# Attention tables of both heads of a block built in its first half, and one of two value copies moved to VectorE

## What is computed

```python
q, k, v = cproj(Wq), cproj(Wk), cproj(Wv)        # complex, 16 heads of 64
qr, kr = q * phase, k * phase                    # rotation by cos and sin tables of the head
E = exp(clip(-mu * |t_i - t_j|, -30, 0))         # decay table of the head
s = Re(qr . conj(kr));  qn = |q|^2;  kn = |k|^2
V = sigma_sq / (2 mu) * (1 - E*E) + eta_sq + gamma_sq
maha = max(qn + E*E*kn - 2*E*s, 0) / V
logits = coef * log1p(maha / nu) - 32 * log(V)   # causal
out = softmax(logits) @ v;  x = x + [Re out, Im out] @ Wo
```

## Time and profile before

| | us |
|---|---|
| median of 3 runs (lowest, highest) | 1714.13 (1711.09, 1719.28) |
| the profiled execution | 1711.93 |
| its span, first to last instruction | 1710.1 |
| busy in the span: PE, DVE, ACT, POOL | 1650.9, 1488.8, 1457.8, 974.7 |
| even halves of the 8 blocks, together | 644.49 |
| odd halves, together | 576.27 |

### The profile page before, as it was taken

The page is one execution under the profiler, slowest core; times in us unless marked ns, Lnnn a source line. Parts: engine busy times, 40 slices in busy tenths (PEclk is TensorE's granted clock), DMA queues, the critical chain, the costliest instruction groups (busy, mean ns, idle before and its releaser), DMA issues. The chain is left out here.

```text
span 1710.1 us, 30987 instructions
## 1 busy us (share of the span) xinstructions
PE 1650.9 (97%) x9690; PEld 1334.7 (78%) x9690; DVE 1488.8 (87%) x3380; ACT 1457.8 (85%) x2924; POOL 974.7 (57%) x826
## 2 busy tenths in 40 slices
PE   5999988999999999999999999999999999999998
PEld 4787866877887888788788778878887887777876
DVE  6878887899899989988998998899899989977675
ACT  6677678999999999999999999999998998766765
POOL 3554556565556556655665566556565655345565
PEclk9999999999999999999999999999999999999999
DMA  6000032232222323232322223232222222100000
GB/s 175 1 1 1 1 102 66 67 80 62 75 60 78 78 59 81 57 87 50 87 66 65 72 72 75 51 87 62 75 66 72 66 63 60 25 1 13 13 8 18
DMA packets 49475, 98.21 MB, mean 57 GB/s; under 512 B 8096, under 2 KB 25760, under 8 KB 49312
## 3 DMA queue, kind: packets, MB, share of 16 engines
q1 hardware_dynamic: 49312, 96.23, 22.0%
HBM read 17.95 MB, written 5.24 MB: 14 GB/s over the span
## 5 line engine op out<-in xcount | busy, mean ns | idle before, releaser
L1482 POOL TENSOR_TENSOR early<-early 128x1024 f32<-128x1024 f32 x127 | 303.4, 2389 | 483.3 <-PE pS L1162 258.2
L654 POOL TENSOR_TENSOR hid_lo_d<-hid_d,hid_hi_d 128x512 fp32r<-128x512 f32 x176 | 231.4, 1315 | 218.7 <-ACT hid_hi_d L559 212.1
L1373 ACT ACTIVATE early<-early,qnorm 128x128 f32<-128x128 f32 (+3 forms) x512 | 246.5, 553 | 71.8 <-DVE early L1564 70.6
L1162 PE MATMUL pS<-early 128*128 128x128 f32 (+3 forms) x1024 | 297.6, 433 | 0.3 <-PEq L105 0.3
L1356 ACT ACTIVATE early<-early,nmax 128x128 f32<-128x128 f32 (+3 forms) x512 | 281.2, 560 | 13.4 <-DVE nmax L1551 12.5
L1560 DVE SCALAR_TENSOR_TENSOR pS<-pS,ek 128x1280 f32<-128x1280 f32 x128 | 191.0, 1492 | 60.7 <-PE pS L1162 59.8
L1162 PEld LDWEIGHTS pS<-early 128*128 128x128 f32 x1024 | 164.7, 191 | 96.0 <-issue 61.4
L1491 POOL TENSOR_TENSOR ek<-early 128x128 f32<-128x128 f32 (+3 forms) x256 | 216.3, 878 | 3.8 <-ACT early L1364 2.9
L1491 POOL TENSOR_TENSOR ek<-decay,early 128x128 f32<-128x128 f32 (+3 forms) x256 | 215.5, 876 | 2.4 <-DVE pS L1560 2.4
L1177 PEld LDWEIGHTS pV<-ones,early 128*128 128x128 f32 x1016 | 134.2, 193 | 60.8 <-issue 60.8
L1207 PE MATMUL pS<-ident,early 128*128 128x128 f32 x1280 | 169.0, 275 | 12.4 <-DVE early L1564 8.3
(11 more groups left out here) (395 smaller groups left out, 3953.3 us busy)
## 6 DMA issues: line engine op xcount, KB each, us to landing
early<-early SPq DMA_DIRECT2D x256, 256.0 KB, 3.6
early<-trig_d SPq DMA_DIRECT2D x64, 64.0 KB, 2.0
trig_d<-early SPq DMA_DIRECT2D x3, 1024.0 KB, 6.9
early<-in_w SPq DMA_DIRECT2D x3, 704.0 KB, 8.8
x_sb<-in_x SPq DMA_DIRECT2D x4, 512.0 KB, 8.4
early<-in_wqk SPq DMA_DIRECT2D x16, 128.0 KB, 3.5
cos<-trig_d SPq DMA_DIRECT2D x32, 64.0 KB, 2.2
sin<-trig_d SPq DMA_DIRECT2D x32, 64.0 KB, 2.0
```

Of the source, the lines that this page charges most:

```text
L654: g.tensor_tensor(hid_lo[:, par], hid[:, par], hid_hi[:, par].bitcast(F32), ALU.subtract).then_inc(lo_done, 1)
L1162: last = pe.matmul(s.pS[:, span(I)], rot[:, I * P:(I + 1) * P], rot[:, N:N + (I + 1) * P], start=True, stop=True)
L1373: last = a.activation(u[:, span(I)], u[:, span(I)], ACT.Relu, bias=qnorm[:, r % 2, I:I + 1])
L1482: g.tensor_tensor(rot[:], by_cos[:], crossed[:], ALU.add).then_inc(S["rot_done"], 1)
```

## The change

Two things change.

First, both heads that come next (the odd one of this block and the even one of the next block) are built in the even half. Each part has now a pair of places, one for each of the two. The decay argument of an even head gets a buffer of its own (`far_even`), because the table `decay[0]` is still in use, and is spread by four DMAs in place of three at r = 8; `lam` of the even heads has two buffers. The parameters are read where they lie, so the copy of them (L1509) is gone. The high part of the weights is cast on VectorE, no longer on ScalarE.

Second, `values_out` on ScalarE copies only the even head's values. The odd head's are copied by VectorE in `values_odd`, at the end of its step, after a wait for ScalarE's copy (`val_done`). TensorE's norms, which write the same banks, wait for both.

```diff
-        FRONT, EXP, EXPAND, LN, MASK = 1, 2, 3, 4, 6
+        FRONT, EXP, HALF, LOW, SQUARE, LN, MASK = (1, 2), (2, 3), (3, 6), (4, 7), (3, 5), (4, 6), (6, 7)
+        WEIGHTS, TRIG, EXPAND = (1, 5), (1, 9), (3, 8)
         def building(part, i, r):
-            if r % B != part:
-                return None
...
+            for off in (1, 2):
+                if r == part[off - 1] and i * 2 + off < H:
+                    return i * 2 + off
+            return None
+            def expand(h):
+                par = h % 2
                 wait(sp, S["decay_done"], h + 1)
+                wait(sp, S["t_done"], 2 * (h - 1) * B)
+                for I in range(TILES - par):
+                    sp.dma_start(decay[par][:, span(I)], far(h)[:, near(I)]).then_inc(expanded[par], 16)
...
                 if live(i, r - 2) and parity(r - 2) == 0:
                     wait(pe, S["val_done"], values_made(i, r - 2))
+                    wait(pe, S["val_odd_done"], values_made(i, r - 2))
...
             def build(part, h):
                 if part == EXP:
-                    a.wait_ge(S["w_in"], h * 16 + 16)
-                    wait(a, S["qk_done"], (h - 1) * B)
-                    a.activation(wqk[par][0][:], wqk_raw[:], ACT.Copy).then_inc(S["w_hi"], 1)
                     a.wait_ge(S["arg_done"], h + 1)
+                    a.activation(far(h), far(h), ACT.Exp).then_inc(S["decay_done"], 1)
...
             def values_out(i, r):
                 a.wait_ge(S["v_done"], values_made(i, r))
-                for h, val in enumerate((val_even[r % B % 3], val_odd[r % B])):
-                    last = a.activation(val[:].rearrange("p (j d) -> p j d", j=TILES),
-                                        s.pV[:].rearrange("p (j h d) -> p h j d", j=TILES, h=2)[:, h], ACT.Copy)
-                last.then_inc(S["val_done"], 1)
+                a.activation(val_even[r % B % 3][:].rearrange("p (j d) -> p j d", j=TILES),
+                             s.pV[:].rearrange("p (j h d) -> p h j d", j=TILES, h=2)[:, 0],
+                             ACT.Copy).then_inc(S["val_done"], 1)
...
+            def build_half(h):
+                v.wait_ge(S["w_in"], h * 16 + 16)
+                wait(v, S["qk_done"], (h - 1) * B)
+                v.tensor_copy(wqk[h % 2][0][:], wqk_raw[:]).then_inc(S["w_hi"], 1)
...
+            def values_odd(i, r):
+                v.wait_ge(S["val_done"], values_made(i, r))
+                wait(v, S["av_done"], i * 16 + r - 7)
+                v.tensor_copy(val_odd[r % B][:].rearrange("p (j d) -> p j d", j=TILES),
+                              s.pV[:].rearrange("p (j h d) -> p h j d", j=TILES, h=2)[:, 1]).then_inc(S["val_odd_done"], 1)
...
+                if live(i, r) and parity(r) == 0:
+                    values_odd(i, r)
```

More of the change, by code:

```diff
@@ L1069, in attention_phase, with lam, far, hp @@
         near = lambda I: slice((TILES - 1 - I) * P, N)
+        def lam(h):
+            return lam1[:] if h % 2 else lam_even[h // 2 % 2]
+        def far(h):
+            return decay[h % 2][:, span(TILES - 1)] if h % 2 or h == 0 else s.far_even
+        def hp(h, k):
+            return s.params[:, h, k:k + 1]
         HALVES = ((slice(0, N), ORDER[:2]), (slice(N, SW), ORDER[2:]))
@@ L1129, in load @@
                     sp.dma_start(sin[par][rows, :], s.trig_d[table, h]).then_inc(trig_in[par], 16)
-            def expand(i, off):
-                h, par = i * 2 + off, off % 2
+            def expand(h):
+                par = h % 2
                 wait(sp, S["decay_done"], h + 1)
-                far = decay[par][:, span(TILES - 1)]
-                for I in range(TILES - 1):
-                    sp.dma_start(decay[par][:, span(I)], far[:, near(I)]).then_inc(S["expanded"], 16)
+                apart(sp, S["sp_passed"])
+                wait(sp, S["t_done"], 2 * (h - 1) * B)
+                for I in range(TILES - par):
+                    sp.dma_start(decay[par][:, span(I)], far(h)[:, near(I)]).then_inc(expanded[par], 16)
             def a_step(i, r):
@@ L1330, in _, with build @@
         def _(a):
-            def build(part, i, off):
-                h, par = i * 2 + off, off % 2
+            def build(part, h):
                 if part == EXP:
-                    a.wait_ge(S["w_in"], h * 16 + 16)
-                    wait(a, S["qk_done"], (h - 1) * B)
-                    a.activation(wqk[par][0][:], wqk_raw[:], ACT.Copy).then_inc(S["w_hi"], 1)
                     a.wait_ge(S["arg_done"], h + 1)
-                    far = decay[par][:, span(TILES - 1)]
-                    a.activation(far, far, ACT.Exp).then_inc(S["decay_done"], 1)
+                    a.activation(far(h), far(h), ACT.Exp).then_inc(S["decay_done"], 1)
                 elif part == LN:
@@ L1343, in build @@
                         a.wait_ge(S["decay_done"], 1)
-                        a.activation(decay2[:], decay[0][:, span(TILES - 1)], ACT.Square).then_inc(S["decay2_done"], 1)
+                        a.activation(decay2[:], far(0), ACT.Square).then_inc(S["decay2_done"], 1)
                     a.wait_ge(S["decay2_done"], h + 1)
-                    wait(a, S["zred_done"], 2 * (h - 1) * B)
-                    a.activation(lam[par][:], decay2[:], ACT.Ln, bias=hp[par][:, A_PLUS_B:A_PLUS_B + 1],
-                                 scale=hp[par][:, NEG_A:NEG_A + 1]).then_inc(S["lnv_done"], 1)
+                    wait(a, S["zred_done"], 2 * (h - (1 if h % 2 else 3)) * B)
+                    a.activation(lam(h), decay2[:], ACT.Ln, bias=hp(h, A_PLUS_B), scale=hp(h, NEG_A)).then_inc(S["lnv_done"], 1)
             def soften(i, r):
@@ L1441, in a_step @@
                 if i == 0 and r == -1:
-                    build(LN, 0, 0)
+                    build(LN, 0)
                 if i == 0 and r == 0:
@@ L1456, in a_step @@
                     if building(part, i, r):
-                        build(part, i, building(part, i, r))
+                        build(part, building(part, i, r))
                 if live(i, r + 2):
@@ L1486, in spread @@
                 wait(g, S["decay_done"], i * 2 + r // B + 1)
-                wait(g, S["expanded"], 48 * (i * 2 + r // B))
+                wait(g, expanded[par], 48 * (i + r // 16 + 1) if par else 64 * (i + r // 16))
                 wait(g, S["norm_done"], n + 1)
@@ L1505, in _ @@
         def _(v):
[L1506 to L1512, removed]
@@ L1544, in peaks @@
-                v.wait_ge(S["lam_done"], i * 2 + r // B + 1)
+                n, h = i * 16 + r, i * 2 + r // B
+                v.wait_ge(S["lam_done"], h + 1)
                 wait(v, S["exp_done"], n)
@@ L1550, in peaks @@
                     for I in pieces:
-                        last = v.tensor_tensor_reduce(z[:, span(I)], u[:, span(I)], lam[par][:, near(I)],
-                                                      hp[par][:, NEG_COEF:NEG_COEF + 1], HIGHEST, ALU.add, ALU.min,
+                        last = v.tensor_tensor_reduce(z[:, span(I)], u[:, span(I)], lam(h)[:, near(I)],
+                                                      hp(h, NEG_COEF), HIGHEST, ALU.add, ALU.min,
                                                       nmax[:, I:I + 1])
@@ L1794, in program @@
         s.hp0 = part(NPAR)
+        s.far_even = part(N)
         s.late_var, s.late_root, s.late_rstd, s.late_shift = (part(2 * TILES) for _ in range(4))
```

91 lines of the change are left out of this document (46 added, 45 removed).

## The result

| | before | after |
|---|---|---|
| median of 4 runs, us (lowest to highest) | 1715.0 (1711.09 to 1719.28) | 1895.91 (1889.75 to 1898.65) |
| profiled span | 1710.1 | 1896.9 |
| even halves together | 644.49 | 842.22 |
| odd halves together | 576.27 | 565.05 |
| mean granted clock | 0.998 | 0.971 |

What follows compares the result with a forecast made beforehand. TensorE was taken to bound the even half before, a ScalarE-VectorE ring with rotate's collision after. Even halves +228.7 us and odd -22.8 on the profiled 1711.93 gave 1917.8, so 1920 us; range 1775 to 1955.

Steps and rivals of the forecast that it cites:

- The ring: Even step: clamp, ScalarE's values copy, VectorE's copy, peaks, next distances form a closed ring of 11.24 us.
- Rotate in peaks: Even step: GpSimd's rotate, asking at 9.98 us, holds a piece of VectorE's peaks for 2.1 us; step 13.3 us.
- Clock: Even step: TensorE idles 3.3 us; a fallen clock delays scores by up to 3.4 us, step again 13.3 us.
- Builds: Even halves: ScalarE's exponential and logarithm add 1.23 us a head, 18.5 us for 15 heads; VectorE's pieces hidden.
- Odd halves: Odd halves without builds: 553.5 us, including 6 us left for late rotates, against 576.3 before.
- the likeliest case: Rotate collides with peaks in most even steps, 13.0 to 13.8 us each: 1900 to 1955 us; chance 0.63.
- the case without a collision: Peaks and rotate miss each other; even steps of 11.24 us, 1788 us in all; chance 0.23.
- the signs: Expected in the profile: even steps 13.3 us, odd 8.7, TensorE under 80% busy in even halves, norms not awaiting odd values.
- The rule of the Trainium skill: GpSimd shares SBUF interfaces with VectorE: two-SBUF-input instructions contend; the new copy, its one input in PSUM, would not.

Runs made afterwards that it cites:

- b_rotate_late: Changed kernel plus one wait: in the even half GpSimd's rotate starts only after the peaks of two steps back; 1795.48 us, ratio 1.047.
- f_after_peaks: Changed kernel with VectorE's copy of the odd values moved behind peaks, its wait for ScalarE's copy kept; 1700.99 us, ratio 0.993.
- a_dve_first: Changed kernel with the value copies' order reversed: VectorE's waits only for TensorE's values, ScalarE's waits for VectorE's; 1697.09 us, ratio 0.989.
- g: Changed kernel with rotate as two instructions of 512 columns in place of one of 1024; 1874.99 us, ratio 1.094.
- c_keep_busy: Changed kernel plus four unused matmuls of 512 columns in TensorE's gap before its transposes in the even half; 1934.85 us, ratio 1.129.

## Why the prediction was right

- **The ring.** Square at 6.69, copy done at 8.19, peaks at 8.82, distances at 11.24: measured 6.69, 8.19, 8.83, and 11.24 in b_rotate_late. VectorE's copy takes 0.69 us, the upper bound, but the next instruction starts 0.61 after its start, so 0.60 was the right figure for the sum; the handover took 0.03. f_after_peaks and a_dve_first show that it is this ring and neither the wait nor the work.
- **Rotate in peaks.** Asked at 9.98, as said; the fourth piece held, step 13.35 for a forecast of 13.3. Steps with an exponential or a logarithm took 13.9 and 14.05, with the third piece held, as said. b and g show it by removing and by halving it.
- **Clock.** Here a step of the prediction failed: "the step is 13.3 again, so this moves the forecast little". I took the clock to fall for all of the work between transposes and scores. In the step shown it fell for some 3 us, the scores came 1.0 us late and not 3.4, and this was enough to free peaks. Five of the 22 short steps had it lower for longer: rotate asked at 12.2 to 12.4 us, and even they took 12.0 to 12.4. With 22 steps of 11.9 us on average, the even halves took 842.2 us for 873.2 forecast. c_keep_busy, with fewer falls, took 872.5; that it lies so near to 873.2 is in part luck, since some 4 us of it are the added matmuls' own.
- **Builds.** 18.5 us in the ring, by 0.52 and 0.71 a piece; b_rotate_late shows 11.76 and 11.94 against 11.24, so 0.52 and 0.70. The pieces on VectorE were hidden.
- **Odd halves.** 553.5 us forecast, 565.05 measured, a term mis-sized by 11.6. The last block's seven odd steps take 67.4 us, not 7 x 8.69 = 60.8, before as after, because of the moments that VectorE makes there for the next layer; I had counted them as builds. The remaining 5 us are late rotates: the odd steps of the first seven blocks together take 11 us more than 8.69 each would make, and I had left 6 for this. Most of it is in 15 steps over 9.1 us; in these rotate starts 1.3 to 1.9 us after distances, as a rule behind the swap DMAs, and a GpSimd piece behind it holds the first or second piece of peaks.
- The two errors, -31.0 and +11.6 us, leave the sum 19 us too high on the profiled execution (1898.65 for 1917.8), and the median at 1896 for 1920; the other 5 us are that the profiled execution lay 2.7 over its median this time and 2.2 under it before.
- How good a hit is that? The mechanism and its terms came out, but that the errors have opposite signs is luck. The median lies just under the 1900 to 1955 of the likeliest case by itself, and inside the stated range only because that reaches down to the case without a collision. A third of the even steps did go without a collision, by way of the lower clock, to which the prediction gave next to nothing.
- Two of the signs did not appear as written. TensorE was busy for 90.24 of 103.46 us and 86.53 of 105.95 us in two of the even halves, 87% and 82%, where under 80% was forecast. Its norms did wait for the odd values, though only in 2 steps, 4.5 us in all.

The rule of the Trainium skill (GPSIMD Engine Reference, Key points) held in its first part: L1565, with two SBUF inputs, was held in 41 steps. For the second there is less: GpSimd ran beside only 2 of the 64 new copies here and 7 in a_dve_first. These, whose one input lies in PSUM, took 0.66 to 0.69 us, no more than the others.

## What to carry to other kernels

Before a copy goes from a loaded engine to a less loaded one, look at what stands behind it in the new queue and for whose late work it waits: a wait ahead of an instruction that feeds the other engine back closes a ring, and its length is the sum of both engines' stretches, whatever their busy shares. The same wait behind that instruction cost at most some 4 us of 1701. Ask also what the move can give: here TensorE set the even step, and the copy's move brought nothing in either order. When an instruction moves in time, ask which transfers and GpSimd instructions now fall beside it; a fixed event at 9.98 us in the step cost nothing as long as the other side was over by 8.4.

## What the runs showed of the hardware

- VectorE's pieces of peaks (L1565, two SBUF inputs) and GpSimd's additions take turns instruction by instruction: a 256-column piece of 0.48 us took 2.60 us behind a GpSimd instruction of 1024 columns and 1.49 us behind one of 512. GpSimd, asking during a piece, got its turn ahead of the next piece that stood ready in VectorE's queue.
- A lower TensorE clock (0.50 granted for some 3 us behind an idle time of 2.77 us) made a step 1.5 us shorter, and four useless matmuls a step, which kept it up in most steps, cost 39 us in all. In three steps with an exponential it made the step 0.6 us longer (14.5 for 13.87), so the gain hangs on where the delayed instruction then falls.
- Best of the kernels run: the tables moved, with either order that opens the ring or with both copies left on ScalarE (1698 us): 1696 to 1701 us, about 1% under the kernel before.
